# Decoder layer on one core: first group's scores placed between half tiles of the MLP product, queries' pieces fetched before the next batch's context

## Chip, cores, metric

One core of one Trainium2 chip. The metric is the device time of one execution in microseconds.

## What is computed

Four sequences (B = 4) of T = 512 tokens with D = 256 features. Three blocks follow each other, each with a residual and a layer norm behind it. Cut to what matters here:

```python
# block 1: a linear recurrence with a gate, then an MLP; x1 is its first residual
mlp = silu(x2n @ w_mlp1.T + b_mlp1) @ w_mlp2.T + b_mlp2
x = layernorm(x + (x1 + mlp))
# block 2: causal cross-attention on the context, 16 heads of 16 features
Q, K, V = proj(x), proj(ctx), proj(ctx)
attn = softmax(where(causal, Q @ K.T / 4, -inf))
x = layernorm(x + (attn @ V) @ wo.T + bo)
# block 3: 48 experts, each takes its best 64 tokens of all 2048, two products and a weighted scatter-add
x = layernorm(x + experts(x))
```

## The kernel before

The program is written by hand, engine by engine: each engine has its own instruction list, and semaphores (class `Signal`: `now(b, k)` is the k-th step of batch b) are all that orders them. Tiles of 128 tokens are called t = 0 to 3.

**Block 1** goes batch by batch. For a batch TensorE makes `expand` (eight hidden tiles of 128 features, each followed by ScalarE's Silu in `hidden`) and `shrink`, the second MLP product: for each token tile eight float32 matmuls (m = 0 to 7) are summed into a 128x256 piece of PSUM banks 6 and 7, tiles 0 and 1 in bank 6, tiles 2 and 3 in bank 7. In the profile a float32 matmul stands as two passes. VectorE then adds the product to the residual (`ln_out`, L1052), takes the statistics (L926, L930); GpSimd makes the root (`root`, L721, L723); VectorE applies the norm (L939). For the last batch (B-1) pieces of the attention of batch 0 already stand between the parts of `expand`: turning of the tokens, projections of keys, queries and values.

**Keys and queries** are kept as exact sums of bf16 pieces (three each; the last step of the queries' split is L1114 on VectorE). They are laid out anew through DRAM: SyncE stores all pieces of a batch (`key_out` L561, `query_out` L565), and fetches them in the layout that the scores need, six DMAs for the keys and six for the queries of each group of four heads (`keys_in`, `queries_in`, L576). `context_in` (L553) and `tokens_in` (L557) load what the next batch is projected from. All of these stand in SyncE's one list, and a wait in it holds everything behind. The destinations KTs and QTs lie over the weights and the hidden tiles of block 1, so groups 0 and 1 may be fetched after `expand` of the last batch, groups 2 and 3 only after `shrink`. GpSimd writes rows that mark the head into KTs (L781, `ones`).

**Block 2** runs in slots (g, j): group g of four heads, key tile j; four groups per batch. For each group the row maxima are needed before the exponentials. So the scores of a group are made one group ahead: eleven banks of scores (`scores`: a causal mask by L1848, then the heads by L1852), in three PSUM buffers; VectorE reduces each bank to its maxima (`maxima`, L1139), then negates them in pieces (`negate`, L1149 to L1156), TensorE turns them (`minus_max`, L1862, four transposes), ScalarE copies them into two rows of QTs (L1534, two copies). In the slots TensorE makes the scores again, shifted by the maxima (`shifted`, L1878), ScalarE the exponentials (L1546) in two PSUM buffers, GpSimd masks the diagonal (L803), TensorE multiplies by the values (`values`, L1891). A table of tasks says what else stands in a slot: in slot (0,0) of batch 0 the turning of the next batch's tokens (L1790, through banks 5 and 7), later GpSimd's sum L796 with the output bias, projections and norms.

For group 0 of batch 0 there is no slot before it. Its scores, maxima and transposes stand in a stretch of their own, between `shrink` of the last batch and the first slot: `ln_out`, eleven banks of scores with their maxima, five idle matmuls (`run_idle`, L1664, they compute nothing that is used), `minus_max`, and a wait for all four of GpSimd's row copies.

**Block 3** streams the experts' weights; the ones that are still missing (`weights`, L528 and L531) are issued by SyncE behind a wait for the last routing logits.

## Time and profile before

| | us |
|---|---|
| median of 3 runs | 656.74 |
| lowest, highest | 655.3, 657.24 |
| the profiled execution's own time | 657.21 |
| its span in the profile | 655.4 |

| engine | busy us | share of the span |
|---|---|---|
| TensorE (PE) | 572.6 | 87% |
| VectorE (DVE) | 383.1 | 58% |
| ScalarE (ACT) | 276.3 | 42% |
| GpSimd (POOL) | 189.2 | 29% |

The median is what counts; the profile is one execution, and its span leaves out what lies around the first and the last instruction (1.8 us here). Busy shares are means over three blocks with different limits, so a stage is read from its own part of the chain and of the timeline. The product of the last batch begins at 166.00 us, the slots of block 2 at 191.02, the routing near 439.

### The profile page before, as it was taken

Reading aid. Unit: us, or ns where it says so; the run is one execution under the profiler, and the core shown is the slowest. Engines: PE = TensorE matmul, PEld = TensorE weight load, DVE = VectorE, ACT = ScalarE, POOL = GpSimd, SP = SyncE. Lnnn points to the kernel's source line nnn. Section 1 sums busy time; section 2 is a strip of 40 time slices with the busy share of each in tenths; the row PEclk is TensorE's granted clock in tenths of the full one; section 3 lists DMA queues with packets and bytes.
Section 4 is the critical chain, followed back from the end, with each engine's and each line's share of the span. In section 5 each row is a group of like instructions: output and inputs, shape, how many; then the busy total and the mean of one; then the engine's idle time right before and its main releaser. Section 6 shows DMA issues by size and latency. Waiting matters only on the chain.

```text
span 655.4 us, 11053 instructions
## 1 busy us (share of the span) xinstructions
PE 572.6 (87%) x3874; PEld 332.1 (51%) x3874; DVE 383.1 (58%) x798; ACT 276.3 (42%) x460; POOL 189.2 (29%) x231
## 2 busy tenths in 40 slices
PE   7899999999979889998999979770399999999993
PEld 3648586664834445564555544330145555555571
DVE  5874747333176757695687758159824334334666
ACT  4260512425046656666766646610043333333304
POOL 3133222060133112121212222210134554452244
PEclk9999999999989979999999979895599999999998
DMA  8796000012530541066114650129269999999974
GB/s 269 220 377 238 0 0 0 1 66 82 179 97 0 174 133 49 7 197 180 38 49 144 219 233 6 59 82 390 122 238 379 391 393 392 399 398 399 329 262 158
DMA packets 43584, 120.40 MB, mean 184 GB/s; under 512 B 6212, under 2 KB 28308, under 8 KB 40468
## 3 DMA queue, kind: packets, MB, share of 16 engines
q1 hardware_dynamic: 38372, 113.20, 47.3%
q0 software_dynamic: 4320, 6.03, 4.2%
q10 hardware_dynamic: 848, 0.60, 0.3%
q8 instruction: 25, 0.41, 0.2%
q14 instruction: 19, 0.16, 0.1%
HBM read 95.88 MB, written 21.83 MB: 180 GB/s over the span
## 4 chain that ended last, share of the span: by engine, by line
PE 73%; DVE 12%; ACT 7%; issue 3%; DMA 3%; POOL 2%; SPq 0%; ACTq 0%; DVEq 0%; POOLq 0%
PE PS L2054 13%; PE PS L1726 8%; PE PS L1735 8%; PE PS L1878 4%; PE PS L1811 4%; PE PS L1891 4%; PE PS L1852 4%; PE PS L2067 4%; PE PS L2088 3%; DVE Mx L1139 3%; ACT arena L1534 2%; PE PS L1830 2%; PE PS L1695 2%; PE PS L1848 2%; PE PS L1803 2%
## 5 line engine op out<-in xcount | busy, mean ns | idle before, releaser
L1139 DVE TENSOR_REDUCE Mx<-PS 128x1 f32<-128x384 f32 (+3 forms) x176 | 104.1, 635 | 41.6 <-PE PS L1852 40.3
L1546 ACT ACTIVATE arena<-PS 128x512 f32<-128x512 f32 (+1 forms) x176 | 90.8, 559 | 49.6 <-PE PS L1878 48.1
L803 POOL TENSOR_SCALAR_AFFINE_SELECT arena<-arena 128x512 f32<-128x512 f32 x64 | 40.9, 639 | 165.9 <-ACT arena L1546 165.9
L1878 PE MATMUL PS<-arena 108*128 108x512 bf16 (+3 forms) x256 | 64.2, 313 | 13.8 <-ACT arena L1546 6.4
L1852 PE MATMUL PS<-arena 96*128 96x128 bf16 (+3 forms) x256 | 64.9, 312 | 0.0
L1726 PE MATMUL PS<-arena 128*128 128x512 f32 x128 | 56.1, 594 | 3.2 <-ACT arena L1451 1.6
L1735 PE MATMUL PS<-arena 128*128 128x256 f32 x256 | 55.9, 379 | 0.0
L1306 DVE COPY X<-PS 128x512 f32<-128x512 f32 x24 | 16.6, 691 | 61.5 <-PE PS L2054 61.5
L1735 PEld LDWEIGHTS PS<-arena 128*128 128x128 f32 x256 | 48.6, 190 | 6.6
L1664 PE MATMUL PS<-ident,identb 128*128 128x512 bf16 x68 | 21.5, 466 | 33.2 <-DVE Y L1264 29.3
L1891 PE MATMUL PS<-arena 128*32 128x128 f32 (+3 forms) x512 | 48.0, 448 | 0.9 <-POOL arena L803 0.9
L1848 PE MATMUL PS<-causal,identb 128*128 128x128 bf16 (+2 forms) x176 | 44.8, 255 | 3.8 <-DVE X L1052 1.7
L1534 ACT ACTIVATE arena<-PS 12x1024 bf16<-12x1024 bf16 x32 | 30.8, 1009 | 39.0 <-PE PS L1862 38.9
L2054 PE MATMUL PS<-ring_a,X 128*64 128x512 f32 x192 | 43.8, 598 | 0.5 <-ACT X L1608 0.5
L1878 PEld LDWEIGHTS PS<-arena 108*128 108x128 bf16 x256 | 22.2, 100 | 43.3 <-issue 15.5
L2054 PE MATMUL PS<-arena,X 128*64 128x512 f32 x192 | 43.8, 598 | 0.1
L1619 ACT ACTIVATE X<-X 128x512 f32<-128x512 f32 x48 | 29.4, 630 | 29.7 <-DVE X L1313 29.7
L1313 DVE TENSOR_TENSOR X<-PS,Y 128x512 f32<-128x512 f32 x48 | 30.9, 685 | 18.2 <-PE PS L2067 18.2
L1726 PEld LDWEIGHTS PS<-arena 128*128 128x128 f32 x128 | 24.2, 190 | 32.5 <-issue 31.9
L1451 ACT ACTIVATE arena<-PS,vec 128x512 f32<-128x512 f32 x16 | 11.4, 775 | 59.5 <-PE PS L1673 59.5
L861 POOL DMA_INDIRECT sums<-row x14 | 22.4, 1602 | 44.7 <-DVE row L1324 32.8
L721 POOL TENSOR_SCALAR ve<-mv 128x4 f32<-128x4 f32 x16 | 3.7, 229 | 107.1 <-DVE mv L930 98.3
(221 smaller groups left out, 965.5 us busy)
## 6 DMA issues: line engine op xcount, KB each, us to landing
ring_a<-experts SPq DMA_DIRECT2D x12, 2048.0 KB, 16.0
arena<-experts SPq DMA_DIRECT2D x12, 2048.0 KB, 18.2
arena<-pieces SPq DMA_DIRECT2D x192, 64.0 KB, 2.3
ring_a<-experts SPq DMA_DIRECT2D x12, 512.0 KB, 15.2
sums<-zrow SPq DMA_DIRECT2D x3, 2048.0 KB, 20.3
arena<-experts SPq DMA_DIRECT2D x12, 512.0 KB, 17.4
pieces<-arena SPq DMA_DIRECT2D x4, 768.0 KB, 3.9
pieces<-ring_a SPq DMA_DIRECT2D x4, 768.0 KB, 3.7
```

The lines of the kernel that those rows point to most:

```text
L803: pool.affine_select(out=pb[j % 2][:, :, 0:P], in_=pb[j % 2][:, :, 0:P], compare_op=ALU.is_ge, fill=0.0, base=0, pattern=[[0, GH], [1, P]] ...
L1139: dve.tensor_reduce(Mx[:, g % 2, i, heads[0]:heads[-1] + 1], bank(score_banks[(g * NSH + u) % 3])[:, 0:len(heads) * w] .rearrange("p (h n) ...
L1313: dve.tensor_tensor(hb[:, a * 512:(a + 1) * 512].rearrange("p (c n) -> p c n", c=8), bank(3 + a).rearrange("p (c n) -> p c n", c=8), b1_s[ ...
L1534: act.activation(QTs[SK:SX, GH * g + 2 * m:GH * g + 2 * m + 2, :], wide(spare(0).bitcast(BF16)[SK:SX, 0:T], 2), ACT.Copy)\
L1546: act.activation(pb[j % 2][:, heads[0]:heads[-1] + 1, 0:w], bank(exp_banks[(g * NSH + n) % 2])[:, 0:len(heads) * w] .rearrange("p (h n) -> ...
L1726: mm = pe.matmul(bank(HIDDEN[m % 4]), wm1_s[:, k, m * P:(m + 1) * P], xT2[:, k, :], start=(k == 0), stop=(k == KT - 1))
L1735: mm = pe.matmul(PS[:, 6 * 512 + t * D:6 * 512 + (t + 1) * D], hid[:, m, t * P:(t + 1) * P], wm2_s[:, m, :], start=(m == 0), stop=(m == MT ...
L1848: pe.matmul(o[:, 0:len(heads) * w].rearrange("p (h n) -> p h n", h=len(heads)) [:, :, i * P:w], identb[:], wide(causal[:], len(heads)), st ...
L1852: mm = pe.matmul(o[:, a * w:(a + 1) * w], QTs[0:SK, g * GH + h, i * P:(i + 1) * P], KTs[0:SK, g * GH + h, 0:w], start=False, stop=True, sk ...
L1878: mm = pe.matmul(bank(exp_banks[(g * NSH + n) % 2])[:, a * w:(a + 1) * w], KTs[0:SX, g * GH + h, j * P:(j + 1) * P], QTs[0:SX, g * GH + h, ...
L1891: mm = pe.matmul(bank(6)[VW * h:VW * (h + 1), j * P:T], Vb[:, j, g * GH + h, :], pb[j % 2][:, h, 0:T - j * P], start=(j == 0), stop=(j == ...
L2054: mm = pe.matmul(bank(1 + n)[CAP * e:CAP * (e + 1), :], xgT[:, k, CAP * e:CAP * (e + 1)], w1_of[u][:, e, k, n * 512:(n + 1) * 512], start= ...
```

## The change

TensorE makes `shrink` of the last batch in half tiles (four of the eight matmuls of a token tile). After the fourth of eight, three score banks of group 0 follow, then a half tile, three banks, a half tile, five banks, a half tile, the transposes of the negated maxima, and the last half tile. The five idle matmuls go. On VectorE `ln_out_norm` is cut in two (`ln_out_statistics` apart), `ln_out` of the last batch moves behind the maxima and the negation, its statistics into slot (0,0) and its norm to the end of slot (0,3). On GpSimd the row copies 2 and 3 and the root move into slots (0,0) to (0,2), each behind the mask; TensorE waits for one copy per group. ScalarE gets an exponential of one column before its first copy of the maxima. SyncE stores the queries before it waits for `expand`, fetches group 0, and only then loads context and tokens of batch 1.

```diff
         exp_first = sb("exp_first", [P, 1])
@@ SyncE
             key_out(0)
-            context_in(1)
-            tokens_in(1)
+            query_out(0)
             sp.wait_ge(b2_out, 16 * NPC)
             sp.wait_ge(m1.s, m1.now(B - 1, MT))
             keys_in(0, 0)
-            query_out(0)
             queries_in(0, 0)
+            context_in(1)
+            tokens_in(1)
             keys_in(0, 1)
             queries_in(0, 1)
@@ GpSimd
-            for g in range(NG):
-                if g == 2:
-                    pool.wait_ge(m2.s, m2.now(B - 1, 1))
+            def own_rows(g):
                 pool.tensor_copy(KTs[SK:SX, GH * g:GH * g + GH, :],
                                  own[SK:SX, :].unsqueeze(2).to_broadcast([SX - SK, GH, T]))\
                     .then_inc(ones, 1)
-            pool.wait_ge(ones, NG)
-            root(ln3, rs3, B - 1, 1 + 2 * TT)
-            pool.wait_ge(rs3.s, rs3.now(B - 1, 2))
+                pool.wait_ge(ones, g + 1)
+            for g in range(2):
+                own_rows(g)
@@ GpSimd, in a slot, behind the mask
+                if (b, g) == (0, 0):
+                    pool.wait_ge(m2.s, m2.now(B - 1, 1))
+                    if j < 2:
+                        pool.wait_ge(msk.s, msk.now(0, j + 1))
+                        own_rows(2 + j)
+                    elif j == 2:
+                        root(ln3, rs3, B - 1, 1 + 2 * TT)
@@ VectorE, in a slot, before its last tasks
+                if (b, g, j) == (0, 0, 0):
+                    ln_out_statistics(B - 1)
+                elif (b, g, j) == (0, 0, TT - 1):
+                    ln_out_norm(B - 1)
@@ VectorE, before the slots
-            ln_out(B - 1)
             spare_banks[:] = 5, 7
             for share in SCORED:
                 for banks in share:
                     maxima((0, 0), banks)
             negate(0, 0)
-            ln_out_norm(B - 1)
+            ln_out(B - 1)
@@ ScalarE
             act_do(late)
+            act.activation(exp_first[:], ident[:, 0:1], ACT.Exp)
             spare_banks[:] = 5, 7
             minus_max(0, 0)
@@ TensorE
+            def shrink_half(b, t, half):
+                per = MT // 2
+                for m in range(half * per, (half + 1) * per):
+                    mm = pe.matmul(PS[:, 6 * 512 + t * D:6 * 512 + (t + 1) * D],
+                                   hid[:, m, t * P:(t + 1) * P], wm2_s[:, m, :],
+                                   start=(m == 0), stop=(m == MT - 1))
+                if (t, half) == (TT - 1, 1):
+                    mm.then_inc(m2.s, 1)
@@ TensorE, in shifted, before the first head of a group of batch 0
+                        pe.wait_ge(ones, g + 1)
@@ TensorE, before the slots
-            shrink(B - 1, range(TT))
+            pe.wait_ge(silu.s, silu.now(B - 1, MT))
+            first_scores = [n for share in SCORED for banks in share for n in banks]
+            spare_banks[:] = 5, 7
+            for t, half in ((0, 0), (0, 1), (1, 0), (1, 1)):
+                shrink_half(B - 1, t, half)
             for k in range(2):
                 pe.wait_ge(*read_by[k])
-            pe.wait_ge(silu.s, silu.now(B - 1, MT))
-            pe.wait_ge(ln3.s, ln3.now(B - 1, 1))
-            read_by.update({0: None, 1: None})
-            for share in SCORED:
-                for banks in share:
-                    scores((0, 0), banks)
-            run_idle(5, 4)
+            read_by.update({0: None, 1: (ln3.s, ln3.now(B - 1, 1))})
+            scores((0, 0), first_scores[0:3])
+            shrink_half(B - 1, 2, 0)
+            scores((0, 0), first_scores[3:6])
+            shrink_half(B - 1, 2, 1)
+            scores((0, 0), first_scores[6:])
+            shrink_half(B - 1, 3, 0)
             minus_max(0, 0)
-            pe.wait_ge(ones, NG)
+            shrink_half(B - 1, 3, 1)
             slots(0, pe_slot, first=True)
```

How the instructions stand on three engines. TensorE, from the second MLP product of the last batch on, before (first fence) and with the change (second):

```order
L1735 MATMUL PS<-arena 128x256 x32
L1848 MATMUL PS<-causal,identb 128x512
L1852 MATMUL PS<-arena 128x128 x4
L1848 MATMUL PS<-causal,identb 128x2x128
L1852 MATMUL PS<-arena 128x256 x2
L1848 MATMUL PS<-causal,identb 128x2x128
L1852 MATMUL PS<-arena 128x256 x2
...
L1848 MATMUL PS<-causal,identb 128x128
L1852 MATMUL PS<-arena 128x512
L1664 MATMUL PS<-ident,identb 128x512 x5
L1862 MATMUL PS<-identb,nst 12x128 x4
L1878 MATMUL PS<-arena 128x512 x2
```

```order
L1752 MATMUL PS<-arena 128x256 x16
L1876 MATMUL PS<-causal,identb 128x512
L1880 MATMUL PS<-arena 128x128 x4
L1876 MATMUL PS<-causal,identb 128x2x128
L1880 MATMUL PS<-arena 128x256 x2
L1876 MATMUL PS<-causal,identb 128x2x128
L1880 MATMUL PS<-arena 128x256 x2
L1752 MATMUL PS<-arena 128x256 x4
L1876 MATMUL PS<-causal,identb 128x128
L1880 MATMUL PS<-arena 128x384
...
L1880 MATMUL PS<-arena 128x512
L1752 MATMUL PS<-arena 128x256 x4
L1890 MATMUL PS<-identb,nst 12x128 x4
L1752 MATMUL PS<-arena 128x256 x4
L1908 MATMUL PS<-arena 128x512 x2
```

The 32 matmuls of the product stood in one piece ahead of all scores; now 16 stand ahead of them, four times 4 between and behind, and the idle matmuls are gone.

SyncE, from the store of batch 0's key pieces on, before and with the change:

```order
L561 DMA pieces<-arena 128x6x512
L553 DMA arena<-ctx_in 128x2x512
L557 DMA Y<-X 128x1024
L576 DMA arena<-pieces 16x2048 x6
L565 DMA pieces<-ring_a 128x6x512
L576 DMA arena<-pieces 16x2048 x42
```

```order
L563 DMA pieces<-arena 128x6x512
L567 DMA pieces<-ring_a 128x6x512
L578 DMA arena<-pieces 16x2048 x12
L555 DMA arena<-ctx_in 128x2x512
L559 DMA Y<-X 128x1024
L578 DMA arena<-pieces 16x2048 x36
```

The store of the queries' pieces (pieces<-ring_a) moved ahead of all fetches (arena<-pieces), and the context and tokens of the next batch (ctx_in, Y<-X) behind the twelve of group 0.

VectorE, from the negation of group 0 to the negation of group 1, before and with the change:

```order
L1149 TENSOR_SCALAR nst<-Mx 128x16
L1151 SCALAR_TENSOR_TENSOR Mr<-Mx,nst 128x16
L1153 SCALAR_TENSOR_TENSOR nst<-Mx,nst 128x16
L1156 TENSOR_TENSOR nst<-Mr,nst 128x16
L926 BN_STATS stats<-X 128x6 x4
L930 BN_AGGR mv<-stats 128x2 x4
L939 TENSOR_SCALAR X<-X,mv,rstd 128x256 x4
L1139 TENSOR_REDUCE Mx<-PS 128x4
L1139 TENSOR_REDUCE Mx<-PS 128x2 x2
L1139 TENSOR_REDUCE Mx<-PS 128x1 x8
L1149 TENSOR_SCALAR nst<-Mx 128x16
```

```order
L1163 TENSOR_SCALAR nst<-Mx 128x16
L1165 SCALAR_TENSOR_TENSOR Mr<-Mx,nst 128x16
L1167 SCALAR_TENSOR_TENSOR nst<-Mx,nst 128x16
L1170 TENSOR_TENSOR nst<-Mr,nst 128x16
L1062 TENSOR_TENSOR X<-PS,X 128x1024
L1153 TENSOR_REDUCE Mx<-PS 128x4
L1153 TENSOR_REDUCE Mx<-PS 128x2 x2
L936 BN_STATS stats<-X 128x6 x4
L940 BN_AGGR mv<-stats 128x2 x4
L1153 TENSOR_REDUCE Mx<-PS 128x1 x8
L1163 TENSOR_SCALAR nst<-Mx 128x16
```

The residual sum (X<-PS,X, before at L1052 ahead of the maxima of group 0) stands behind the negation, the statistics behind three maxima of group 1, and the norm further down, in slot (0,3).

## Rows read from the trace of the kernel before

**Rows 1.** Page, part 4: the chain that ended last, by engine.
```profile
PE 73%; DVE 12%; ACT 7%; issue 3%; DMA 3%; POOL 2%; SPq 0%; ACTq 0%; DVEq 0%; POOLq 0%
```

**Rows 2.** Chain that ended last, 158 to 212 us: start us, us, what.
```profile
180.09 1.24 DVE X L1052
...
191.85 1.28 ACT L1546
```

**Rows 3.** Timeline, 160 to 192 us: start us, us, engine line op out<-in xcount [idle before <-releaser].
```profile
166.00 13.98 PE L1735 MATMUL PS<-arena 128*128 128x256 f32 x64
...
180.04 3.73 POOL L781 CAST arena<-own 12x2048 bf16<-12x2048 f32 x2 [13.44 <-PE PS L1735]
...
181.67 0.38 PE L1848 MATMUL PS<-causal,identb 128*128 128x512 bf16 x1 [1.70 <-DVE X L1052]
...
188.55 0.18 DVE L1149 TENSOR_SCALAR nst<-Mx 128x16 bf16<-128x16 f32 x1
...
189.19 1.41 DVE L926 BATCH_NORM_STATS2 stats<-X 128x6 f32<-128x256 f32 x4
...
189.90 1.93 ACT L1534 ACTIVATE arena<-PS 12x1024 bf16<-12x1024 bf16 x2 [26.59 <-PE PS L1862]
...
191.02 0.59 PE L1878 MATMUL PS<-arena 108*128 108x512 bf16 x2 [1.15 <-issue]
...
191.97 1.06 PE L1790 MATMUL PS<-ident,Y 128*128 128x128 f32 x8
```

**Rows 4.** Timeline, 193 to 203 us, slot (0,0) of batch 0.
```profile
193.98 1.94 DVE L1139 TENSOR_REDUCE Mx<-PS 128x4 f32<-128x512 f32 x3
...
195.75 0.34 PE L1878 MATMUL PS<-arena 108*128 108x384 bf16 x1 [0.61 <-ACT arena L1546]
...
197.33 0.22 PE L1848 MATMUL PS<-causal,identb 128*128 128x128 bf16 x1
...
200.99 2.35 POOL L796 TENSOR_TENSOR X<-X,row 128x1024 f32<-128x1024 f32 x1
...
202.02 1.36 DVE L1149 TENSOR_SCALAR nst<-Mx 128x16 bf16<-128x16 f32 x1
```

**Rows 5.** Page, part 2, and windows: granted clock in tenths; busy us, PEclk, DMA share, GB/s.
```profile
PEclk9999999999989979999999979895599999999998
...
core 0: us, PE busy (x) PEld busy (x) DVE busy (x) ACT busy (x) POOL busy (x), PEclk, DMA share, GB/s
...
186.00:188.00 2.00, 2.00 (x7) 0.67 (x7) 2.00 (x5) 0.00 (x0) 0.00 (x0) 0.50 0.48 143
```

**Rows 6.** Timeline of VectorE (first) and of SyncE's DMA issues around the queries' pieces.
```profile
161.79 1.23 DVE L1114 TENSOR_TENSOR ring_a<-ring_a 128x1024 bf16<-128x1024 f32 x1 [1.12 <-ACT ring_a L1521]
...
166.75 0.43 SPq L565 DMA_DIRECT2D pieces<-ring_a  x1
170.64 20.32 SPq L576 DMA_DIRECT2D arena<-pieces  x42
```

**Rows 7.** DMA issues from 159, 163, 166.7 and 173.4 us: KB each, median us to landing.
```profile
Y<-X SPq DMA_DIRECT2D x1, 512.0 KB, 6.5
...
arena<-pieces SPq DMA_DIRECT2D x6, 64.0 KB, 3.2
...
pieces<-ring_a SPq DMA_DIRECT2D x1, 768.0 KB, 3.8
...
arena<-pieces SPq DMA_DIRECT2D x12, 64.0 KB, 2.3
```

**Rows 8.** Timeline of TensorE: the first of the four transposes of a group.
```profile
205.07 0.22 PE L1862 MATMUL PS<-identb,nst 128*12 128x128 bf16 x1
...
235.09 0.22 PE L1862 MATMUL PS<-identb,nst 128*12 128x128 bf16 x1 [1.61 <-DVE nst L1156]
...
250.00 0.22 PE L1862 MATMUL PS<-identb,nst 128*12 128x128 bf16 x1
...
295.90 0.22 PE L1862 MATMUL PS<-identb,nst 128*12 128x128 bf16 x1 [0.73 <-DVE nst L1156]
...
309.58 0.22 PE L1862 MATMUL PS<-identb,nst 128*12 128x128 bf16 x1
```

More of the change, by code:

```diff
@@ L182, in build @@
         rden = sb("rden", [P, TT, GH])
+        exp_first = sb("exp_first", [P, 1])
         used = [0]
@@ L1053, in ln_out, with ln_out_statistics, ln_out_norm @@
                                   ALU.add).then_inc(ln3.s, 1)
-            def ln_out_norm(b):
+            def ln_out_statistics(b):
                 dve.wait_ge(ln3.s, ln3.now(b, 1))
                 statistics(ln3, X, b * TT, b, 1)
+            def ln_out_norm(b):
                 norm(ln3, rs3, X, lambda t: X[:, b * TT + t, :], b * TT, b)
@@ L1083, in _ @@
                 ln_out(b)
+                ln_out_statistics(b)
                 ln_out_norm(b)
@@ L1086, in _ @@
             ln_out(B - 2)
+            ln_out_statistics(B - 2)
             ln_out_norm(B - 2)
@@ L1869, in shifted @@
                 for n, heads in enumerate(SHARED[j], FIRST[j]):
+                    if (b, j, heads[0]) == (0, 0, 0):
+                        pe.wait_ge(ones, g + 1)
                     if j == 0 and heads[0] % 2 == 0:
@@ L1977, in _ @@
             pe.wait_ge(ln3.s, ln3.now(B - 2, 1))
-            shrink(B - 1, range(TT))
+            pe.wait_ge(silu.s, silu.now(B - 1, MT))
[3 more added lines that the diff above has]
+                shrink_half(B - 1, t, half)
             for k in range(2):
                 pe.wait_ge(*read_by[k])
-            pe.wait_ge(silu.s, silu.now(B - 1, MT))
-            pe.wait_ge(ln3.s, ln3.now(B - 1, 1))
-            read_by.update({0: None, 1: None})
-            spare_banks[:] = 5, 7
-            for share in SCORED:
-                for banks in share:
-                    scores((0, 0), banks)
-            run_idle(5, 4)
+            read_by.update({0: None, 1: (ln3.s, ln3.now(B - 1, 1))})
[5 more added lines that the diff above has]
+            shrink_half(B - 1, 3, 0)
             minus_max(0, 0)
-            pe.wait_ge(ones, NG)
+            shrink_half(B - 1, 3, 1)
             slots(0, pe_slot, first=True)
```

## Prediction

> **What bounds the kernel now.** I read the page first, then the chain of waits around the place of the change, then the timeline of each engine there. The chain that ended last is TensorE for 73% of the span [rows 1], so time is to be found where TensorE waits for others. Just behind the last second MLP product the chain leaves TensorE: for VectorE's residual sum L1052 (1.24 us), and later for ScalarE's table load at the first exponential (1.28 us) [rows 2]. The timeline shows the whole stretch: the product L1735 ends at 179.98, and the first shifted scores L1878 start at 191.02 [rows 3]. In these **11.04 us** TensorE only makes the eleven score banks of group 0, each paced by a maximum on VectorE, five idle matmuls and four small transposes.
>
> **The order of TensorE.** The change puts this serial stretch into the product. The product is 64 passes in 13.98 us [rows 3], 0.218 us each, so a half tile (4 matmuls of two passes) is 1.75 us. All times that follow are on the clock of the profiled execution, with the product begun as before at 166.0. Four half tiles end at 173.0.
> First three score banks: between 191.02 and 191.97 TensorE issued two shifted banks and one score bank [rows 3], so a bank of many heads is at most 0.5 us; I take 1.2 for the three. They end at 174.2, half tile (2,0) at 175.95. Their maxima cost 1.94 us for three [rows 4] and are done by 175.7, so they gate nothing. Three banks of one wide head at 0.3 us (estimate from the same rows): to 176.85. Half tile (2,1): to 178.6. Then five banks on three PSUM buffers: the first three run at once, the fourth needs the maximum of the first, the fifth that of the second. A maximum is 0.65 us for 512 columns [rows 4], so about 0.5 for 384. The fifth bank starts at 180.2 and ends at 180.6, after 0.6 us of waiting. Half tile (3,0): to 182.35. The last maximum ends at 182.2, the four small steps of the negation take 0.64 us (188.55 to 189.19) [rows 3], so the transposes L1862 go at 183.0 and take 0.4: 183.4. Half tile (3,1): to 185.2. Under it ScalarE makes its two copies L1534 (1.93 us) [rows 3], ready at 185.4; the first shifted scores need only the first of them. So the slots start at **185.2 instead of 191.0, 5.8 us earlier**. The five idle matmuls are gone; they covered the wait for the negation, most of which half tile (3,0) covers now. If a half tile covered nothing, its wait would be back, 0.6 us at a time.
>
> **Are the queries' pieces there at 173.0?** The queue is reordered for this. Before, the queries' store went out at 166.75, and their pieces from 170.64 on [rows 6]. Now the store follows VectorE's last step on them, which ends at 163.02 [rows 6]: store at 163.05, landed 3.8 us later [rows 7], 166.85. The six key pieces go meanwhile. Issues cost 20.32 us for 42, 0.48 each [rows 6]: six query pieces leave by 169.8 and land 2.3 us later, or 3.2 as the pieces did that shared the queue with bigger loads [rows 7]: **172.1 to 173.0**. I take a stall of 0, since these are rows of the same transfers. The lower end is 0 too; for the upper I give the store the 6.5 us of the tokens [rows 7]: 169.55 + 2.9 + 3.2 = 175.65, a stall of 2.7.
> Behind these in the queue: context and tokens of batch 1 leave at about 170, not 159. The tokens' reader L1790 comes at about 186; with 6.5 us they are there by 178: nothing. Twelve pieces of group 1 leave by 177, wanted at 185.6: nothing. Groups 2 and 3 wait for the product's end, now 185.2 instead of 180.0; group 2 lands by 185.2 + 5.8 + 2.3 = 193.3 and is wanted some 15 us after the slots' start: nothing. What these lose in slack would be a stall of scores if the queue were slower by 6 us.
>
> **VectorE in slot (0,0).** The residual sum (1.24 us) [rows 2] now stands at the head of the slot, 0.1 to 1.35 us after its start. The first transposes L1790 begin 0.95 us after the start and take 1.06 for both halves [rows 3]; only the second half needs the sum, at 1.5: no stall. The maxima follow. Behind three of them stand the statistics, 1.41 us and four aggregates more, 1.9 us together [rows 3]. Before, statistics and norm stood ahead of those maxima, which began at 193.98, and TensorE's fourth bank of that batch (197.33, 6.3 us after the start) found its maximum done [rows 4].
> **ScalarE.** The table load now comes at about 163.4, where ScalarE is idle for 26.6 us [rows 3]: its cost there is nothing. The fifth shifted bank (195.75, after a wait of 0.61 for an exponential) [rows 4] can go 3.3 instead of 4.7 us after the start, and the fourth score bank at 4.9. But the three maxima end at 4.0, the statistics hold VectorE until 5.95, and the first maximum of the next four ends at 6.45. TensorE stalls 1.6 us there. The 1.4 us of the table load are lost again, and TensorE is **0.3 us later** than before, counted from the slots' start (estimate).
> **GpSimd.** A row copy is 1.87 us (3.73 for two) [rows 3]. Copies 2 and 3 now follow the masks of j = 0 and 1; those masks stay ahead of their values by 0.8 us or more: nothing. The root follows the third mask, some 10.3 us after the start, and pushes the bias sum L796 from 200.99 (10.0 us after) to 11.6: it ends at 14.0. Before, the negation's first step took 1.36 us instead of 0.18, up to the end of that sum [rows 4]; I let it wait again. With half a microsecond for the rest it ends at 14.6 to 14.9, while TensorE wants it at 14.35 (205.07 [rows 8] is 14.05 after the start, and 0.3). Between 0, if the steps get in ahead of the sum, and 0.6: I take **0.5**, since the same two instructions met before. The norm goes to the end of slot (0,3), where there are no maxima: nothing; beyond that place it could hold those of group 2, by under 1 us.
>
> **The sum:** 5.8 - 0.3 - 0.5 = **5.0 us**. The profiled run took 657.21 us, 0.47 above the median of 656.74: 652.2 from the one, 651.7 from the other; I take 652.0. Nothing behind has a date of its own: the weights of the expert stage that are still missing are issued behind a wait for the routing logits, so the shift goes to the end whole.
>
> **Rivals.**
> (a) *The pieces come late.* For: at the upper end of the landing the margin is nothing. Against: nothing big shares the queue any more. With 1 to 2.7 us: 653 to 654.7.
> (b) *VectorE's queue gives back more.* If sum and statistics (1.24 + 1.9) lay on the path whole: 652.0 + 3.1 - 0.3 = 654.8. Against: before, as much stood ahead of the maxima.
> (c) *The clock helps.* It fell to 0.50 (1.2 GHz) at 186 after TensorE's thin stretch, and falls again in later slices [rows 5]. Group 3 of batch 0, with such a fall, took 14.9 us between its transposes (235.09 to 250.00), the same group of batch 1 13.7 (295.90 to 309.58) [rows 8]: 1.2 us. If one or two of the three later falls of the attention go away, or my 0.8 us of losses do not come: 650.2.
> (d) *Slower: the clock falls inside the product.* Place: the second half of the product, between 173 and 185, where my order leaves TensorE idle 1.3 us in pauses. The granted clock fell before only where TensorE had been waiting in short turns [rows 3, 5]. Price: at 1.2 GHz each half tile takes 1.75 us more, and the first group 1.2 more. Three half tiles use up the gain; all four and the group give 652.0 + 7.0 + 1.2 = 660.2.
> The Trainium skill (TensorE: Matmul & The Clock Gate, HAM oscillation) says that matmuls in bursts with waits between them fall back to the low clock again and again; that speaks against splitting a dense product by scores that wait and against dropping the idle matmuls. By that rule the time would be that of (d), by the rows above the forecast.
> Against (d): 1.3 us of pauses in 12, none over 0.7, where before 1.7 us stood empty at once and each maximum held TensorE again.
> (e) *Nothing comes of it,* because a later stage waits for a transfer with its own date: 656.7. Against: the wait for the logits.
>
> **Chances.** Forecast within 1.3 us: 0.65. (a) 0.09, (b) 0.09, (c) 0.11, (d) 0.03, (e) 0.03. A measurement of this kernel tells 0.3%, 2 us (below 654.8 here), from no change. Faster by more takes the forecast, (c), (a) and half of (b): 0.91; same 0.06; slower 0.03. The range takes in (c) and most of (a) and (b): 649.6 to 654.9.
>
> **What would show it.** In the new profile: the product in one piece of 16 matmuls and four of 4; the first score bank within 0.3 us of the fourth half tile's end (later: a); no idle matmuls behind the last score; the first shifted scores 19.2 us after the product's start, 25.0 before; the table load near 163; a TensorE wait for a maximum of about 1.6 us some 5 us into the slots (far more: b); the transposes of group 1 14.9 us after the slots' start, 14.05 before; granted clock 1.00 from 173 to 186 (less: d). The forecast is wrong if the slots start less than 4 us earlier, or if the groups behind take over 1 us longer at full clock.

## The result and the profile after

| | before | with the change |
|---|---|---|
| median, us | 657.24 (11 runs) | 650.28 (11 runs) |
| lowest of the runs, us | 655.22 | 648.11 |
| ratio, 95% interval | | 0.9908 (0.9887 to 0.9929) |
| profiled execution: own time, span | 657.21, 655.4 | 652.62, 650.8 |

By the ratio the change saves 0.92%, some 6.0 us (4.7 to 7.4). A second comparison gave 652.26 against 656.19 us, ratio 0.9926 (0.9897 to 0.9955), so 4.9 us. Two executions were disturbed and stand in no ratio: one of the kernel before (715.23 us, still counted in its median above) and one of an experiment below (e5_both, 988.83 us at a granted clock of 0.555). Lines have moved: the half tiles are L1752, a score bank L1876 and L1880, maxima L1153, negation L1163 to L1170, transposes L1890, shifted scores L1908, residual sum L1062, bias sum L799, masks L806, values L1921.

The page of the profile after, part 4: the chain is TensorE's still, a little more so [rows 1].

```profile
PE 74%; DVE 12%; ACT 6%; issue 3%; POOL 2%; DMA 1%; ACTq 0%; DVEq 0%; POOLq 0%; SPq 0%
```

The timeline of the profile after, on all engines, from the product to the transposes of group 1 (start us, us, engine, line, operation, count, and the idle time before with its releaser). It answers to [rows 2, 3, 4].

```profile
163.39 1.28 ACT L1606 ACT_TABLE_LOAD   x1
...
166.05 7.07 PE L1752 MATMUL PS<-arena 128*128 128x256 f32 x32
...
172.96 0.38 PE L1876 MATMUL PS<-causal,identb 128*128 128x512 bf16 x1
...
174.07 1.89 PE L1752 MATMUL PS<-arena 128*128 128x256 f32 x8
...
176.02 0.22 PE L1876 MATMUL PS<-causal,identb 128*128 128x128 bf16 x1
...
176.24 0.22 PE L1876 MATMUL PS<-causal,identb 128*128 128x128 bf16 x1
...
176.47 1.89 PE L1752 MATMUL PS<-arena 128*128 128x256 f32 x8
...
180.11 1.89 PE L1752 MATMUL PS<-arena 128*128 128x256 f32 x8
...
182.36 0.39 PE L1890 MATMUL PS<-identb,nst 128*12 128x128 bf16 x4 [0.35 <-DVE nst L1170]
...
182.68 1.99 PE L1752 MATMUL PS<-arena 128*128 128x256 f32 x8
...
184.51 0.60 PE L1908 MATMUL PS<-arena 108*128 108x512 bf16 x2
...
184.78 1.22 DVE L1062 TENSOR_TENSOR X<-PS,X 128x1024 f32<-128x1024 f32 x1 [2.48 <-PE PS L1752]
...
188.51 1.39 DVE L936 BATCH_NORM_STATS2 stats<-X 128x6 f32<-128x256 f32 x4
...
190.93 0.23 PE L1876 MATMUL PS<-causal,identb 128*128 128x128 bf16 x1 [1.29 <-DVE Mx L1153]
...
196.14 2.40 DVE L1170 TENSOR_TENSOR nst<-Mr,nst 128x16 bf16<-128x16 f32 x1
196.14 2.35 POOL L799 TENSOR_TENSOR X<-X,row 128x1024 f32<-128x1024 f32 x1
...
199.34 0.22 PE L1890 MATMUL PS<-identb,nst 128*12 128x128 bf16 x1 [0.77 <-DVE ring_a L1117]
```

The 64 passes that stood as one row are now 32 and four times 8. The first score bank comes at 172.96, right behind the fourth half tile, and the slots start at **184.51, 6.51 us earlier** than 191.02. The rows behind show what was given back: a score bank that waited 1.29 us for a maximum at 190.93, behind the statistics (188.51) on VectorE; and the transposes at 199.34, 0.77 us late: the last step of the negation took 2.40 us beside GpSimd's bias sum of 2.35, and VectorE's next step (L1117), which ends TensorE's wait, came behind it. The exponentials' table load stands at 163.39, where ScalarE had nothing to do.

The queue, SyncE alone, with landing times from the same view of DMA issues as [rows 7] (the store's, and that of the pieces issued from 167.5 to 170.8 us). It answers to [rows 6, 7].

```profile
163.10 0.36 SPq L567 DMA_DIRECT2D pieces<-ring_a  x1
163.64 7.07 SPq L578 DMA_DIRECT2D arena<-pieces  x12
170.75 0.42 SPq L555 DMA_DIRECT2D arena<-ctx_in  x1
...
pieces<-ring_a SPq DMA_DIRECT2D x1, 768.0 KB, 4.9
...
arena<-pieces SPq DMA_DIRECT2D x7, 64.0 KB, 2.3
```

The queries' store went out at 163.10 as forecast, and landed after 4.9 us, not 3.8. The query pieces could leave from 168.0 on, the last at about 170.3, and with 2.3 us to land it was there at 172.6, some 0.4 us before TensorE asked.

The windows of the profile after, of the product's second half and of three stretches of the attention (busy us, then granted clock, DMA share, GB/s), which answer to [rows 5]:

```profile
core 0: us, PE busy (x) PEld busy (x) DVE busy (x) ACT busy (x) POOL busy (x), PEclk, DMA share, GB/s
173.00:186.00 13.00, 12.38 (x75) 9.00 (x73) 8.18 (x17) 2.94 (x4) 0.00 (x0) 1.00 0.41 123
216.00:220.00 4.00, 3.50 (x18) 2.67 (x17) 1.09 (x2) 3.03 (x5) 0.00 (x0) 0.60 0.70 237
376.00:384.00 8.00, 7.36 (x48) 4.44 (x46) 2.85 (x6) 5.65 (x9) 0.64 (x1) 0.58 0.35 147
408.00:420.00 12.00, 10.01 (x53) 3.50 (x54) 0.68 (x2) 6.24 (x13) 2.54 (x4) 0.57 0.00 0
```

The clock stayed up through the interleaved half (1.00). It still falls to 1.2 GHz at three places of the attention, and the windows of 4 to 12 us that hold them show 0.57 to 0.60. Placed by the transposes of the groups, one of them shows against [rows 8]:

```profile
215.11 0.22 PE L1890 MATMUL PS<-identb,nst 128*12 128x128 bf16 x1 [1.61 <-DVE nst L1170]
...
230.68 0.22 PE L1890 MATMUL PS<-identb,nst 128*12 128x128 bf16 x1 [1.61 <-DVE nst L1170]
...
243.38 0.22 PE L1890 MATMUL PS<-identb,nst 128*12 128x128 bf16 x1
```

Group 2 to 3 of batch 0 took 15.57 us (215.11 to 230.68), where the kernel before took 14.0; group 3, which had the fall before and took 14.9, took 12.70. In the whole profile the shift is 6.51 us at the slots' start, 5.96 at the transposes of group 2 (215.11 against 221.07), 6.74 at the last transposes of the attention (405.42 against 412.16), 5.13 at the logits (434.12 against 439.25), and 4.6 at the end. So 1.6 us of the shift were lost in one stretch: from the last transposes to the logits it took 28.70 us where the kernel before took 27.09. The granted clock was 0.50 there from 408 to 418 us in the profile after, and below 1.00 only from about 418 to 421 in the profile before.

### The profile page after: what moved, and what is told of

It reads as the page before. It is cut to its first block, busy times and chain, and to the rows that moved or that the text cites. A ratio compares the mean times of both kernels' runs of the same rounds, so it can differ in the third digit from the quotient of the medians.

```text
span 650.8 us, 11045 instructions
## 1 busy us (share of the span) xinstructions
PE 571.2 (88%) x3869; PEld 332.0 (51%) x3869; DVE 383.4 (59%) x798; ACT 276.2 (42%) x461; POOL 189.4 (29%) x231
## 4 chain that ended last, share of the span: by engine, by line
PE 74%; DVE 12%; ACT 6%; issue 3%; POOL 2%; DMA 1%; ACTq 0%; DVEq 0%; POOLq 0%; SPq 0%
PE PS L2086 13%; PE PS L1744 9%; PE PS L1763 6%; PE PS L1921 5%; PE PS L1908 5%; PE PS L1880 4%; PE PS L1839 4%; PE PS L2099 4%; PE PS L2120 3%; DVE Mx L1153 3%; PE PS L1858 2%; PE PS L1713 2%; PE PS L1876 2%; PE PS L1752 2%; ACT arena L1551 2%
## 5 line engine op out<-in xcount | busy, mean ns | idle before, releaser
L1153 DVE TENSOR_REDUCE Mx<-PS 128x1 f32<-128x384 f32 (+3 forms) x176 | 104.0, 635 | 46.7 <-PE PS L1880 45.4
L806 POOL TENSOR_SCALAR_AFFINE_SELECT arena<-arena 128x512 f32<-128x512 f32 x64 | 40.9, 639 | 181.3 <-ACT arena L1563 174.3
L1908 PE MATMUL PS<-arena 108*128 108x512 bf16 (+3 forms) x256 | 64.1, 315 | 11.7 <-ACT arena L1563 5.6
L1880 PE MATMUL PS<-arena 96*128 96x128 bf16 (+3 forms) x256 | 62.8, 305 | 0.0
L1921 PE MATMUL PS<-arena 128*32 128x128 f32 (+3 forms) x512 | 49.0, 457 | 0.6 <-POOL arena L806 0.6
L1876 PE MATMUL PS<-causal,identb 128*128 128x128 bf16 (+2 forms) x176 | 44.2, 251 | 2.9 <-DVE Mx L1153 2.5
L1908 PEld LDWEIGHTS PS<-arena 108*128 108x128 bf16 x256 | 22.1, 99 | 42.1 <-issue 16.6
L1763 PE MATMUL PS<-arena 128*128 128x256 f32 x192 | 41.9, 379 | 0.0
L1744 PEld LDWEIGHTS PS<-arena 128*128 128x128 f32 x128 | 24.2, 190 | 32.4 <-issue 31.9
L1763 PEld LDWEIGHTS PS<-arena 128*128 128x128 f32 x192 | 36.5, 190 | 5.0
L1626 ACT ACTIVATE X<-PS 128x256 f32<-128x256 f32 x24 | 9.2, 384 | 59.3 <-PE PS L2072 59.3
```

The source lines that it names most:

```text
L806: pool.affine_select(out=pb[j % 2][:, :, 0:P], in_=pb[j % 2][:, :, 0:P], compare_op=ALU.is_ge, fill=0.0, base=0, pattern=[[0, GH], [1, P]] ...
L1153: dve.tensor_reduce(Mx[:, g % 2, i, heads[0]:heads[-1] + 1], bank(score_banks[(g * NSH + u) % 3])[:, 0:len(heads) * w] .rearrange("p (h n) ...
L1744: mm = pe.matmul(bank(HIDDEN[m % 4]), wm1_s[:, k, m * P:(m + 1) * P], xT2[:, k, :], start=(k == 0), stop=(k == KT - 1))
L1763: mm = pe.matmul(PS[:, 6 * 512 + t * D:6 * 512 + (t + 1) * D], hid[:, m, t * P:(t + 1) * P], wm2_s[:, m, :], start=(m == 0), stop=(m == MT ...
L1876: pe.matmul(o[:, 0:len(heads) * w].rearrange("p (h n) -> p h n", h=len(heads)) [:, :, i * P:w], identb[:], wide(causal[:], len(heads)), st ...
L1880: mm = pe.matmul(o[:, a * w:(a + 1) * w], QTs[0:SK, g * GH + h, i * P:(i + 1) * P], KTs[0:SK, g * GH + h, 0:w], start=False, stop=True, sk ...
```

## Experiments

Each is the change with one edit. "To group 2" is the time from the slots' start (first L1908) to the first transposes of group 2, in that kernel's profile: 30.05 us before, 30.60 in the change. It sorts out what happens at the start from the falls of the clock further on. Where one profile is all there is of a stretch, it says nothing of the spread from run to run.

### Interleaving undone (e6_whole), and with idle matmuls (e9_whole_idle)

```diff
-            scores((0, 0), first_scores[0:3])
-            shrink_half(B - 1, 2, 0)
-            scores((0, 0), first_scores[3:6])
...
+            scores((0, 0), first_scores)
             minus_max(0, 0)
```

> The change with its interleaving alone undone: the whole product, then eleven score banks, then the transposes, still without idle matmuls; the residual sum stays behind the negation, queue, table load and GpSimd as in the change. Theory (the gain comes from scores under the product): the scores begin at 180.0 instead of 181.7 of before, the slots start at 189.2 to 189.5 (191.0 before, 184.5 with the change), so the time is some 4.8 us above the change and about 1.6 below before. Rival (the gain comes from the moved residual sum, the queue and the table load, and the interleaving only shifts waits): the slots start within 1 us of 184.5.

Timeline of TensorE in it, the first score and the two rows at the end of the stretch:

```profile
180.05 0.38 PE L1876 MATMUL PS<-causal,identb 128*128 128x512 bf16 x1
...
187.69 0.39 PE L1890 MATMUL PS<-identb,nst 128*12 128x128 bf16 x4 [2.09 <-DVE nst L1170]
189.23 1.01 PE L1908 MATMUL PS<-arena 108*128 108x512 bf16 x2 [1.15 <-issue]
```

The slots start at 189.23, as the theory said. So of 6.51 us, 1.8 are the residual sum taken out of the way with the other edits that stayed in (191.02 to 189.23; the first score alone comes 1.62 us earlier, 180.05 against 181.67), and **4.7 are the interleaving** (189.23 to 184.51). The rival falls. The time did not follow: 659.93 us median of ten runs (654.34 to 661.07), ratio to before 1.0044 (1.0014 to 1.0073), so slower than the kernel before, though its stage is shorter. The profile is of a run of 654.42. Two more kernels asked why.

> The kernel with the interleaving alone undone, and the five idle matmuls of before put back behind its scores. Without them its ten runs lay from 654.3 to 661.1 us, with the granted clock between 0.961 and 0.948 over the span. Theory A (the wait for the negation with nothing on TensorE makes the clock fall there, and in more places behind): the runs gather at 654 to 656, granted clock 0.96. Theory B (the spread has to do with where the falls of the attention land, not with this place): the runs spread as before from 654 to 661. In both the slots start at 189.3, or up to 1 us later if the clock falls as it did in the kernel before.

```diff
             scores((0, 0), first_scores)
+            run_idle(5, 4)
             minus_max(0, 0)
```

654.25 us median (652.34 to 658.26), ratio 0.9966 (0.9929 to 1.0003): by the ratios, taken in two comparisons, the five idle matmuls are worth about 0.8% in the serial form, with the slots at the same place (189.19). The intervals of the two don't touch. Six of its ten runs gathered between 652.3 and 654.3, but four lay near 657.5, so neither theory holds alone. The kernel before, which has its idle matmuls, spreads too: 6 of the 13 runs beside this one took 658.7 us or more.

This kernel is also the better measure of what the interleaving is worth in time, since it has idle matmuls where the change has a half tile. Its ratio of 0.9966 against 0.9908 and 0.9926 of the change makes 0.4 to 0.6%, or 2.6 to 3.8 us, with intervals that touch or overlap. The 4.7 us are shown at the slots' start, in the profiles; in the time they are not shown whole.

> The kernel with the interleaving alone undone, a second look. Its first profile belongs to one of the fastest of its runs (654.4 us). If this one is near 660, its extra 5 to 6 us should lie in groups of the attention at a granted clock of 0.50, 1.2 to 2 us each (theory: falls of the clock), not in one wait. Rival: one stage, the experts' for instance, is longer as a whole.

657.2 us this time. Windows of the second profile of the serial form without idle matmuls (first) and of the one with them:

```profile
184.00:188.00 4.00, 1.73 (x11) 0.65 (x10) 3.90 (x10) 0.00 (x0) 0.00 (x0) 0.76 0.55 143
188.00:190.00 2.00, 0.85 (x5) 0.29 (x3) 0.70 (x1) 1.75 (x2) 0.00 (x0) 0.50 0.57 148
190.00:192.00 2.00, 2.00 (x11) 1.55 (x10) 0.66 (x1) 1.26 (x3) 0.00 (x0) 0.50 0.56 150
```

```profile
184.00:188.00 4.00, 2.81 (x16) 0.99 (x15) 3.90 (x10) 0.00 (x0) 0.00 (x0) 1.00 0.50 139
188.00:190.00 2.00, 0.85 (x4) 0.38 (x4) 0.72 (x1) 1.93 (x2) 0.00 (x0) 0.88 0.52 133
190.00:192.00 2.00, 2.00 (x12) 1.85 (x11) 0.69 (x1) 1.42 (x3) 0.00 (x0) 0.50 0.65 162
```

Without them TensorE was busy 1.73 us of 4 ahead of the transposes, and the clock fell there, before the slots, in this run (0.76, then 0.50 to 192); with them it fell about 189.7. The first group then took 17.94 us between its transposes against 17.54, and a later group 14.86 against 12.70 with another fall. Those two groups hold 2.6 of the 3.6 us between the two profiles (655.4 and 651.8), so most of the extra time lies in groups with falls, as the theory said. A run near 660 was not caught in a profile, and why falls behind this place come more often without the idle matmuls stays open.

### The queue's old order (e1_queue)

```diff
             key_out(0)
-            query_out(0)
+            context_in(1)
+            tokens_in(1)
             sp.wait_ge(b2_out, 16 * NPC)
             sp.wait_ge(m1.s, m1.now(B - 1, MT))
             keys_in(0, 0)
+            query_out(0)
             queries_in(0, 0)
-            context_in(1)
-            tokens_in(1)
```

> The change with SyncE's old order: context and tokens of batch 1 first, the queries' store behind the keys. Theory: the pieces of group 0 land at about 175.5, the first score waits for them from 173.0 on, and everything behind starts 2.5 us later (slots at 187.0 instead of 184.5). Rival (the fetch is hidden anyway): no wait, slots at 184.5.

Timeline of TensorE in it, and the window behind its wait:

```profile
175.29 0.38 PE L1876 MATMUL PS<-causal,identb 128*128 128x512 bf16 x1 [2.14 <-DMA arena<-pieces]
...
176.39 3.48 PE L1752 MATMUL PS<-arena 128*128 128x256 f32 x8
179.67 0.31 PE L1876 MATMUL PS<-causal,identb 128*128 128x128 bf16 x1
...
188.51 0.60 PE L1908 MATMUL PS<-arena 108*128 108x512 bf16 x2
...
176.00:180.00 4.00, 4.00 (x16) 2.95 (x14) 1.88 (x3) 0.00 (x0) 0.00 (x0) 0.57 0.45 130
```

The wait is there (2.14 us, for the fetch), but the slots start at 188.51, **4.0 us late, not 2.5**. The rest is the next half tile: 3.3 us (176.39 to 179.67) instead of 1.72 (174.07 to 175.79 in the change), because the clock fell to 0.50 within 0.2 us of its start, after the pause. This is the forecast's rival (d) at its place, for one half tile and near its price (1.6 us against 1.75), set off by a late fetch. To group 2 it is 30.59, so nothing changed up to there. The one time is 656.77 us, no better than the kernel before beside it (656.11).

### No early table load (e2_no_table)

```diff
-            act.activation(exp_first[:], ident[:, 0:1], ACT.Exp)
```

> The change without the early exponential of one column. Theory (VectorE's statistics hold TensorE at the same place, so the early load gives nothing): the load of 1.28 us is back before the first exponential, the wait of TensorE for the first maximum behind the statistics shrinks from 1.29 us by the same amount, and slot group (0,0), 14.83 us from the slots' start to the transposes of group 1, stays within 0.3 us. Rival (the load is a term of its own): that stretch grows by 1.3 us.

Timeline of ScalarE and TensorE in it:

```profile
184.63 0.60 PE L1907 MATMUL PS<-arena 108*128 108x512 bf16 x2
...
185.10 1.28 ACT L1563 ACT_TABLE_LOAD   x1 [0.26 <-PE PS L1907]
...
189.00 0.34 PE L1907 MATMUL PS<-arena 108*128 108x384 bf16 x1 [0.61 <-ACT arena L1563]
...
191.50 0.23 PE L1875 MATMUL PS<-causal,identb 128*128 128x128 bf16 x1 [0.75 <-DVE Mx L1153]
...
199.08 0.22 PE L1889 MATMUL PS<-identb,nst 128*12 128x128 bf16 x1
```

The load is back at 185.10; TensorE waits for an exponential (0.61), and the wait for the maximum behind the statistics falls from 1.29 to 0.75. From the slots' start to the transposes of group 1 it is 14.45 us, to group 2 30.61, against 14.83 and 30.60. But the negation's last step did not meet the bias sum here (it took 0.19 us at 196.72, and the sum began at 197.25). The second profile of the change (below), where they did not meet either, has 14.00 and 30.16. So by one profile each the early load is worth some 0.45 us where the two don't meet, and nothing where they do; the forecast of nothing holds for the first profile alone. The one time is 649.4 us.

### Statistics and bias sum moved (e3_stats, e4_bias, e5_both, e5_again)

```diff
@@ e3, e5
-                if (b, g, j) == (0, 0, 0):
+                if (b, g, j) == (0, 0, 1):
                     ln_out_statistics(B - 1)
@@ e4, e5
+                if (b, g, j) == (0, 0, TT - 1):
+                    with_bias(0)
                 for name, c, k in steps[0] + steps[1] + steps[2] + steps[3]:
-                    if name == "bias":
+                    if name == "bias" and (b, g) != (0, 0):
                         with_bias(c)
```

> The change with the statistics of the last batch at the end of slot (0,1) instead of (0,0), so behind the four maxima that TensorE waits for. Theory: the wait of 1.29 us goes, and the stretch from the slots' start to the transposes of group 1 falls from 14.83 us to 13.5 or less. Since the negation then comes ahead of GpSimd's bias sum, the wait of 0.77 us may go with it: down to 12.8, unless the mask of the fourth key tile (198.45) then holds TensorE. Rival (TensorE's own work bounds the stretch): within 0.3 us of 14.83.

It started at 184.96, reached the transposes of group 1 12.55 us later, and group 2 after 29.14: both waits are gone, and one that the expectation named has come. The one time is 648.28 us. Timeline of TensorE, the values of slot (0,3):

```profile
199.59 0.43 PE L1921 MATMUL PS<-arena 128*32 128x128 f32 x8 [1.27 <-POOL arena L806]
```

> The change with GpSimd's bias sum of batch 0 alone moved behind the mask of slot (0,3); the statistics stay in (0,0). Theory: the negation's last step, 2.40 us beside the bias sum in the change, falls to 0.2, TensorE's wait of 0.77 us ahead of the transposes of group 1 goes, and the stretch from the slots' start to them falls from 14.83 to 14.06 us; TensorE still waits 1.29 us behind the statistics. Rival (the last step was slow for another reason): 14.8.

14.01 us to group 1, 30.16 to group 2, and one time of 650.94 us. That looks like the theory, but a second profile of the change (below) has 14.00 and 30.16 with the bias sum in its old place: there the negation's last step began 0.02 us before the sum and took 0.19. So this one profile can't tell what the edit gives. The last step did not fall to 0.2 here either: it began at 196.15, 0.01 us behind a mask of GpSimd (0.64 us), and took 0.67. The collision with the sum is worth up to 0.77 us at group 1 and 0.44 at group 2 (30.60 against 30.16), and is a matter of some hundredths whether it happens.

> The change with the statistics of the last batch at the end of slot (0,1), and GpSimd's bias sum of batch 0 behind the mask of slot (0,3) instead of (0,2). With the statistics moved alone, TensorE's values waited 1.3 us for the mask of the fourth key tile, which stood behind the bias sum. Theory: that wait goes too; from the slots' start to the transposes of group 2, 29.14 us with the statistics moved alone and 30.60 in the change, falls to about 28. Time 1.5 to 2.5 us under the change. Rival (the bias sum now meets the maxima of group 2 and the norm): 29.1 or more.

> Statistics at the end of slot (0,1) and bias sum behind the mask of slot (0,3), again, since the profile of the first job was of a disturbed run (987 us at a granted clock of 0.555). Theory: slots from 184.5 to 185.0, about 12.8 us from there to the transposes of group 1 (14.83 in the change), about 28 to those of group 2 (30.60), no wait of TensorE for a mask; 2 to 3 us under the change. Rival: 29.1 or more to group 2, within 1.5 us of the change.

The second profile, timeline of TensorE:

```profile
184.56 0.60 PE L1910 MATMUL PS<-arena 108*128 108x512 bf16 x2
...
197.11 0.22 PE L1892 MATMUL PS<-identb,nst 128*12 128x128 bf16 x1
```

12.55 us to group 1 and 28.71 to group 2, **1.5 to 1.9 below the two profiles of the change and 1.3 below the kernel before**; the wait for the mask is gone. The 28.71 lie between the 28 of the theory and the 29.1 of the rival. Times: a median of 646.99 us of the other four runs, ratio 0.9831 (0.9762 to 0.9900), in the first comparison, 647.69 with 0.9888 (0.9843 to 0.9933) in the second. The change beside it in the second gave 0.9926, so it is 2.5 us better by the ratios, with intervals that overlap: it has the lowest medians of all versions, but that it beats the change is shown for the stage and not for the time.

### Idle matmuls ahead of three groups' transposes (e7_idle)

```diff
-                pe.wait_ge(mneg.s, mneg.now(b, 4 * (g + 1)))
                 o = take(0, nte, nte.now(b, 2 * g + 2)).bitcast(BF16)
+                run_idle({(0, 2): 6, (0, 3): 6, (3, 0): 11}.get((b, g), 0), 5)
+                pe.wait_ge(mneg.s, mneg.now(b, 4 * (g + 1)))
```

> The change with idle matmuls ahead of three groups' transposes, where TensorE waits for the negation: six each for groups 2 and 3 of batch 0 (waits of 1.61 us), eleven for group 0 of batch 3 (wait of 2.83 us). Theory (the falls behind those waits come from them): the groups that took 15.57 and 16.51 us in the change take 14.0 and 14.8, the time falls by 1 to 3 us and the spread of the runs narrows. Rival (the falls are not set by these waits): the groups keep falls, here or one group on, and the time stays within 1 us or rises by up to 1 us, since idle matmuls that outlast the wait delay the transposes.

Timeline of TensorE, the change's transposes of group 0 of batch 3 (first), and this kernel's of groups 0 and 1 of batch 3:

```profile
362.11 0.22 PE L1890 MATMUL PS<-identb,nst 128*12 128x128 bf16 x1
```

```profile
362.90 0.22 PE L1891 MATMUL PS<-identb,nst 128*12 128x128 bf16 x1
...
376.76 0.22 PE L1891 MATMUL PS<-identb,nst 128*12 128x128 bf16 x1 [2.93 <-DVE nst L1170]
```

651.03 us median of four, ratio 0.9898 (0.9825 to 0.9970): no difference to the change. The groups that had taken 15.57 and 16.51 us took 14.02 and 14.65. But the group that ends with the eleven matmuls grew from 13.45 us to 15.82. The expectation had their place wrong: the wait of 2.83 us stands ahead of group 1 of batch 3 (375.88 in the change), and ahead of group 0 there is none (362.11). So they covered no wait and delayed the transposes by 2.4 us, their own length, and the wait of group 1 stayed (2.93). The shorter group behind it is therefore not their doing.

The first half of the theory, for the waits of 1.61 us, is consistent with this, not shown: five kernels without these idle matmuls (e2, e3, e5, e6, e9) took 14.02 us there too. A long wait alone does not bring a fall either: e3_stats has the same wait ahead of group 1 of batch 3, and its clock stayed up behind it. Its timeline of TensorE and its window there:

```profile
373.70 0.22 PE L1890 MATMUL PS<-identb,nst 128*12 128x128 bf16 x1 [2.84 <-DVE nst L1170]
...
376.00:380.00 4.00, 2.45 (x23) 1.79 (x21) 2.15 (x4) 3.51 (x8) 0.49 (x1) 1.00 0.25 103
```

### The change again (after_again)

> The change itself once more, beside the kernels that build on it. Expected 650 to 651 us, slots from 184.5 in its profile, 14.83 us from there to the transposes of group 1, with other falls of the clock in the attention than in the first profile if these are a matter of chance.

652.26 us (647.99 to 654.2), above the 650 to 651 expected; slots at 184.58, to group 1 14.00, to group 2 30.16. The falls sit at the same groups as in the first profile (15.54 and 16.44 us), so their place was not a matter of chance in these two. Behind the last transposes there is no loss here (27.09 us to the logits, as before), and the logits come at 432.04, 7.21 us earlier than before. From the logits to the end this profile needs 218.4 us, the first 216.7, before 216.2: a spread of 2 us that belongs to the expert stage and that none of these kernels touches.

## Why the prediction was right, step by step

- **The schedule of TensorE.** Forecast 185.2 for the slots, measured 184.51. The order came as worked out; the term that was too large is a score bank of one wide head, 0.22 us from one to the next (176.02 to 176.24) where I took 0.3, and 0.32 us instead of 0.4 for the transposes. Together with first banks 0.1 us shorter, and transposes that could start 0.15 us sooner behind the last bank, this makes most of the 0.7 us. TensorE's pauses from 173 to 186 us were 0.6 us together (12.38 busy of 13.00), where I took 1.3.
- **The pieces at 173.0.** Forecast a stall of 0 with a landing from 172.1 to 173.0. There was none, but with 0.4 us of margin, so with some luck: the store took 4.9 us beside the key fetches, not the 3.8 I took for it, though within the 6.5 of the upper end. e1_queue shows what lateness costs: its wait and a fallen clock.
- **Residual sum, statistics, table load.** Forecast a wait of 1.6 us behind the statistics, measured 1.29. The first maximum behind them is done about where I had it: the score bank that waits for it starts at 190.93, 6.42 us after the slots' start, against 6.45. That the statistics are what holds TensorE is shown by e3_stats. That the table load is lost there holds only where the bias sum collides (e2_no_table); else it is worth 0.45. The residual sum, put at no stall, held a weight load of TensorE for 0.30 us (at 186.06), which the wait behind the statistics takes up.
- **Bias sum.** Forecast 0.5, between 0 and 0.6; two profiles of the same kernel show 0.77 and 0. The whole loss to group 1 was forecast as 0.8, and is 0.78 in one profile and -0.05 in the other. That the first agrees is luck: of its two terms the 0.3 came out as about 0, and the 0.5 as 0.77. In the kernel before it was the first step of the negation that met the sum, in the change the last.
- **The sum.** Forecast 5.0 us. At the transposes of group 2, ahead of the falls, it is 5.96 (before 221.07, after 215.11), and 6.3 in the second profile. The ratios say 6.0 and 4.9. Size and sign are right. In the first profile the missing microsecond is 0.7 us of the slots' start, mostly the score banks and the steps behind the last of them, and 0.25 of the losses (0.55 at group 2, where I took 0.8). The bias sum is no part of it there, since it cost more than forecast; in the second profile it cost nothing. From there on the profile behind does not keep a fixed shift, as the forecast had it: 6.74 us at the last transposes, 5.13 at the logits, 4.6 at the end.
- **Rivals.** (a) did not come, by little. (b) did not come. (c) and (d) were the same thing as a source of spread: the profile kept three falls, at 1.55 to 1.8 us by the groups (15.57 against 14.02; 16.51 against 14.70, a group that had a shorter fall itself) and 1.6 behind the last transposes (28.70 against 27.09). All are more than the 1.2 I priced. That price was read against group 3 of batch 1 (13.7), which does other work; against the same group of batch 0 without a fall (12.70) it is 2.2. So the median of 650.28 near the number of (c) does not show (c). (d) at its own place came only with the old queue. (e) is refuted: the logits came 5.13 us earlier, and the end 4.6.
- **Chances.** The forecast, (c), (a) and half of (b) add up to 0.90, not 0.91.

The rule of the Trainium skill in (d) (TensorE: Matmul & The Clock Gate, HAM oscillation), that bursts with waits between them fall back to the low clock again and again, did not come true in the change: granted clock 1.00 from 173 to 186 us. What I drew from it on dropping idle matmuls fits the serial form (e6_whole against e9_whole_idle, 1.0044 against 0.9966). It does not fit the change, since half tiles stand where they stood.

## What to carry over

A serial stretch in which two engines take turns can be hidden by cutting a long product of the same engine into pieces of about the length of the other engine's turn; count the banks in flight and place a piece ahead of each wait. Then look at what decides when its inputs are there, because a late fetch cost its wait here and, on TensorE, the slow clock behind it (4.0 us for a wait of 2.14). Work that is moved out of the way lands in some other engine's queue: ask for each piece which wait it now stands ahead of, and put it behind the results that are waited for (here 1.5 to 1.9 us up to group 2). And before idle matmuls are put ahead of a wait, read from the timeline that the wait is there.

## What the runs showed of the hardware

- A pause of 2.14 us in a dense float32 product was followed by the clock at 1.2 GHz, and by a half tile of 3.3 instead of 1.72 us (e1_queue). Pauses of up to 0.35 us in the same product were not (182.36 in the change, granted clock 1.00 from 173 to 186). A pause of 2.84 us in the attention was not either in e3_stats (373.70, granted clock 1.00 from 372 to 380), where the change had the clock at 0.66 and then 0.50 behind the same pause of 2.83 us (375.88, windows 376 to 380 and 380 to 384).
- The same pause and the same work behind it took different times: the group behind 2.83 us of waiting took 16.51 us in the change and 14.62 in e5_again (372.48 to 387.10), where the granted clock was 0.63 from 372 to 376 and 0.94 from 376 to 380.
- Leaving out five idle matmuls in a stretch of waits moved the ratio of a kernel to the one before by 0.8% of 656 us (1.0044 against 0.9966, two comparisons), although its own stage started at the same time to 0.04 us.
- A 128x16 step on VectorE (two inputs in SBUF) took 2.40 us when it began with a 2.35 us sum on GpSimd (both at 196.14), and 0.19 us when it began 0.02 us before it (196.21 and 196.23). With 0.01 us between them it went either way: 2.40 us in e1_queue (200.14 and 200.15), 0.19 in e6_whole (202.12 and 202.13).
- A table load took 1.28 us and the next activation began 0.01 us behind it (163.39 to 164.68).
